# A seven-product feed-forward for the second batch, with GpSimd adding the W quarters

## The chip, the cores and the metric

The kernel runs on one NeuronCore of a Trainium2 chip. The metric is the device time of one execution in microseconds (us); lower is better. PE is TensorE, DVE is VectorE, ACT is ScalarE, POOL is GpSimd and SP is the engine whose queue issues most of the DMAs. L12 is line 12 of the kernel file; a number above 1875 is always a line of the changed file.

## The reference, cut to what matters

Two batches of 1024 tokens with 2048 features go through a quantised cross-attention product and then a feed-forward product with LoRA terms. Both have the same residual form.

```python
x = x + fake_quant(layernorm(x)) @ fake_quant(ctx)             # per batch: (1024 x 2048) @ (2048 x 2048)
y = layernorm(x)
x = x + y @ W + bias + (y @ A_eff[b].T) @ B_eff[b].T + (y @ A_shared.T) @ B_shared.T
# W: 2048 x 2048 f32; eight gate groups, four for each batch; rank 32
```

The feed-forward product must be more exact than one f16 product. Both y and W are split into a high and a low f16 part, and three products are summed: high*high, high*low and low*high.

## The kernel before

A batch is 8 token tiles of 128 rows. All work is written out by hand for each engine, with semaphores between them; each engine runs its list in order. One batch has two phases of 4 column blocks (512 columns, `NBLK`). Phase one is the attention product, one bf16 matmul for each of 16 k steps (L1006). Phase two is the feed-forward: for each column block and each token tile `base_group` issues 16 k steps of three f16 matmuls (L1191, L1192, L1193), and `delta` adds two matmuls for the LoRA term (L1202, L1203). That makes 4 x 8 x 16 x 3 = 1536 main matmuls in a batch, all 128x128 by 128x512. `lora_in` (L1214) makes the rank-64 product of y four times in a batch, with 32 matmuls of 256 columns each.

Each token tile has its own of the 8 PSUM banks. `evict1` (L1464) and `evict2` (L1503) on DVE add a finished bank, scaled, to the residual `x2` in SBUF.

y is made tile by tile. DVE takes statistics (L1471, L1476), an inverse root (L1344 to L1347) and the scaled rows into `xn` (L1486); ACT copies the high part (`split_hi`, L750); DVE subtracts to get the low part (`low2`, L1496); SP issues a transposing DMA of each into `lhs` (L357, L365).

W comes in pieces of 128 x 2048 f32 (1 MB) through `stage`, which holds two pieces. The load of a piece waits until the piece two places earlier has been converted (`load_w`, L458). ACT writes the high part into `ring` (L774) and DVE the low part (L1450). One column block is 4 pieces, and each of the 16 pieces is loaded once in a batch. The LoRA rows `b_st` take the same way through `stage` (L482, L484, L781, L1456).

POOL adds the attention's column term to the residual (L613), loads a row of bias into `bias_sb` for each column block (L631), adds it to the 8 tiles (L638), and issues the stores of the output (L644, L699). Its list for a block is: bias row, eight additions, eight stores.

Of the kernel before, what the change touches and what calls it, by code (L numbers as in the profile page):

```python
# [15 lines left out]
P = 128  # L16
# [13 lines left out]
def build(nc, x, ctx_in, par, w, bias, lora_a, lora_b, lora_as, lora_bs, out):  # L30
# [20 lines left out]
    bg_scratch = nc.dram_tensor("bg_scratch", (RANK, NGATE, D), F32, kind="Internal").ap()  # L51
    bg_rows = bg_scratch.rearrange("(q h r) g o -> (h r g) q o", h=2, q=NQ // 2)
# [7 lines left out]
    with ExitStack() as es:  # L60
# [18 lines left out]
        sc = sb("sc", [P, 116], F32)  # L79
# [53 lines left out]

        def w_first(g):
            return slot(g % 2)
# [29 lines left out]
        NEG_HALF = sc[:, 104:106]  # L165

# [89 lines left out]
        stored = sem("stored")  # L256

# [83 lines left out]

        block = es.enter_context(nc.Block())

        @block.sync
        def _(sp):
# [41 lines left out]
            def load_gates(b):  # L387

                if b == 0:
                    for n in range(NBLK):  # L390
                        sp.wait_ge(ag_dram[n], 16)
                    sp.wait_ge(be_full, 6)
                else:
                    sp.wait_ge(base_done, NBLK * TILES)
                    sp.dma_start(ash(b), lora_as).then_inc(sh_again, 16)
                sp.dma_start(a_gates, ag_scratch[:, b * GPB:(b + 1) * GPB, :, :]).then_inc(ag_in, 16)
# [96 lines left out]

            for b in range(NBATCH):
                if b:
                    load_ctx(b, 0, [0, 1])
                    for t in range(5):
                        turn_next(b, t)
                    load_ctx(b, 0, [2])
                    turn_next(b, 5)  # L500
                    load_ctx(b, 0, [3])
                    turn_next(b, 6)
                    turn_next(b, 7)
                    load_ctx(b, 1, [0, 1])
                    load_gates(b)
                    load_ctx(b, 1, [2, 3])
                    with sp.Fori(2, NBLK) as j:
                        ctx_block(b, j)
                w_block(b, 0)
# [31 lines left out]
        def _(pool):  # L541
# [73 lines left out]
            def store_a(b, gs):  # L615

                for g in gs:
                    pool.wait_ge(a_lo, b * (GPB + 1) + g + 2)
# [28 lines left out]
            bias_row = bias.rearrange("(a n) -> a n", a=1)  # L647
            for b in range(NBATCH):
# [12 lines left out]
                else:  # L661
# [6 lines left out]
                    add_column(b, 3)  # L668
                add_bias(b, 0, blk2(b, 0), False)
# [33 lines left out]
        def _(act):  # L703
# [154 lines left out]
            def shared_hi(b):  # L858
                if b:
                    act.wait_ge(sh_again, 16)  # L860
# [5 lines left out]
                for n in range(2):  # L866
                    last = act.activation(a_f16[:, n, :, RANK:R2], ash(b), ACT.Copy, scale=SA)
# [13 lines left out]


# [16 lines left out]
            for b in range(NBATCH):  # L899
# [37 lines left out]
                for j in range(1, NBLK):  # L937
# [12 lines left out]
                    if j == 2:  # L950
                        gate_hi(b, 2)
                        gate_hi(b, 3)

# [42 lines left out]
        def _(pe):  # L996
# [220 lines left out]

            for b in range(NBATCH):
                if b == 0:
                    first_block()  # L1220
                for j in range(0 if b else 1, NBLK):
                    first_by_tile(b, j)
                k = blk(b, 1, 0)
# [75 lines left out]
        def _(dve):  # L1299
# [159 lines left out]
            def evict1(b, j, t):  # L1459
                dve.wait_ge(psum_full, blk(b, 0, j) * TILES + t + 1)  # L1460
                if b:
# [3 lines left out]
                                         op0=ALU.mult, op1=ALU.add).then_inc(evicted, 1)  # L1465

# [60 lines left out]
            def evict_and_convert(b, j):  # L1527
# [23 lines left out]
                if b == 0 and j == 1:  # L1551
                    power_a()
                if b == 0 and j == 2:
# [11 lines left out]
                if j == 2:  # L1565
                    gate_low(b, 2)
# [47 lines left out]
            def shared_low(b):  # L1614

                dve.wait_ge(a_hi, b * (GPB + 1) + 1)
                for n in range(2):
                    last = dve.scalar_tensor_tensor(out=a_f16[:, n, :, R2 + RANK:2 * R2], in0=ash(b), scalar=SA,
# [3 lines left out]
            def gate_low(b, g):  # L1622

                dve.wait_ge(a_hi, b * (GPB + 1) + g + 2)
# [104 lines left out]

            for b in range(NBATCH):  # L1730
                for j in range(NBLK - 1):
# [6 lines left out]
                    if b == 0 and j == 2:  # L1738
                        max_of_first_w(2)

# [86 lines left out]
                if b + 1 < NBATCH:  # L1827
                    steps[0] += LAP * (NBLK - 3)
                    for t in range(LNL, TILES):
# [46 lines left out]
```

## Time and profile before

| what | before |
|---|---|
| median of 3 runs | 1051.88 us (1051.62 to 1055.79) |
| profiled execution | 1053.82 us, span 1052.3 us |
| PE busy | 996.7 us, 95% of the span |
| DVE / ACT / POOL busy | 537.4 / 305.5 / 209.8 us |
| DMA moved | 181.70 MB |
| first feed-forward matmul of the second batch | 676.73 us |

The span is the time from the first to the last instruction in the profile. A matmul's entry overlaps the next one's, so the distance between starts tells the pace, not the duration shown.

### The profile page before, as it was taken

The numbers are of one execution on the slowest core, as the hardware profiler recorded it, in microseconds if no ns is written. First come the engines' busy times: TensorE is split into PE (matmuls) and PEld (weight loads), VectorE is DVE, ScalarE is ACT, GpSimd is POOL, SyncE is SP. The second block draws the span as 40 slices with busy tenths as digits, with TensorE's granted clock in tenths as the row PEclk, the third lists the DMA queues.
The fourth block names the chain that finished last, engine by engine and source line by source line (L and its number), as shares of the span: only waits on it lengthen the run. The fifth ranks groups of instructions, "written<-read, shape, count | busy, mean of one in ns | idle before, by whom it ended". The sixth has DMA issues, their size and how long they took to land.

```text
span 1052.3 us, 12182 instructions
## 1 busy us (share of the span) xinstructions
PE 996.7 (95%) x4736; PEld 470.0 (45%) x4759; DVE 537.4 (51%) x761; ACT 305.5 (29%) x234; POOL 209.8 (20%) x231
## 2 busy tenths in 40 slices
PE   2899999999999999999999999989999999999996
PEld 1364444444544444444444344445544444444442
DVE  7766869878364565454414756787442023014010
ACT  4684423444031142132213521353330021012000
POOL 3011000111014013113311634320204004003110
PEclk9999999999999999999999999999999999999998
DMA  9699862679465245447699743665824025014010
GB/s 364 235 312 390 319 271 46 170 143 214 153 221 201 79 160 189 164 156 199 253 293 292 290 181 129 145 143 125 229 101 160 31 98 162 20 33 156 10 46 24
DMA packets 124392, 181.70 MB, mean 173 GB/s; under 512 B 96064, under 2 KB 96064, under 8 KB 111808
## 3 DMA queue, kind: packets, MB, share of 16 engines
q1 hardware_dynamic: 109600, 118.25, 37.9%
q0 software_dynamic: 13600, 58.73, 15.2%
q10 hardware_dynamic: 1152, 4.19, 1.0%
q8 instruction: 25, 0.41, 0.2%
q14 instruction: 15, 0.12, 0.0%
HBM read 128.72 MB, written 29.36 MB: 150 GB/s over the span
## 4 chain that ended last, share of the span: by engine, by line
PE 67%; DVE 11%; DMA 8%; issue 5%; ACT 5%; SPq 2%; POOL 2%; DVEq 0%; POOLq 0%; ACTq 0%
PE psum L1191 16%; PE psum L1193 16%; PE psum L1192 16%; PE psum L1006 14%; DMA stage<-in_w 2%; PE psum L1214 2%; PE psum L1071 1%; DVE hl L1496 1%; DMA stage<-in_ctx_in 1%; DMA xn<-in_x 1%; SPq L365 1%; DMA lhs<-hl 1%; DMA bias_sb<-in_bias 1%; DVE ring L1450 1%; PE psum L1202 1%
## 5 line engine op out<-in xcount | busy, mean ns | idle before, releaser
L1191 PE MATMUL psum<-ring,lhs 128*128 128x512 f16 x1016 | 386.4, 380 | 9.1 <-issue 6.0
L1192 PE MATMUL psum<-ring,lhs 128*128 128x512 f16 x1016 | 386.3, 380 | 0.0
L1193 PE MATMUL psum<-ring,lhs 128*128 128x512 f16 x1016 | 386.3, 380 | 0.0
L1006 PE MATMUL psum<-ring,lhs 128*128 128x512 bf16 x1002 | 228.7, 384 | 4.5 <-DVE ring L1416 2.0
L1191 PEld LDWEIGHTS psum<-ring,lhs 128*128 128x128 f16 x1016 | 99.6, 98 | 131.0 <-issue 8.4
L1006 PEld LDWEIGHTS psum<-ring,lhs 128*128 128x128 bf16 x1024 | 100.9, 99 | 127.8 <-issue 7.4
L1193 PEld LDWEIGHTS psum<-ring,lhs 128*128 128x128 f16 x1016 | 99.6, 98 | 120.7 <-issue 1.4
L1192 PEld LDWEIGHTS psum<-ring,lhs 128*128 128x128 f16 x1016 | 99.7, 98 | 119.6 <-issue 1.4
L1503 DVE SCALAR_TENSOR_TENSOR x<-psum,sc,x 128x512 f32<-128x512 f32 (+1 forms) x64 | 45.3, 745 | 180.4 <-PE psum L1203 179.5
L638 POOL TENSOR_TENSOR x<-x,bias_sb 128x512 f32<-128x512 f32 (+1 forms) x64 | 89.0, 1416 | 185.7 <-ACT x L915 123.6
L774 ACT ACTIVATE ring<-stage,sc 128x2048 f16<-128x2048 f32 x32 | 63.6, 1999 | 207.7 <-PE psum L1193 159.9
L1450 DVE SCALAR_TENSOR_TENSOR ring<-stage,sc,ring 128x2048 f16<-128x2048 f32 x32 | 75.0, 2349 | 78.1 <-ACT ring L774 74.8
L762 ACT ACTIVATE ring<-stage,pats_sb,sc 128x2048 int16<-128x2048 f32 x30 | 62.5, 2089 | 88.1 <-DMA stage<-in_ctx_in 47.2
L644 POOL DMA_DIRECT2D out<-x x48 | 26.7, 556 | 237.2 <-DVE x L1503 213.6
L1464 DVE SCALAR_TENSOR_TENSOR x<-psum,sc,x 128x512 f32<-128x512 f32 x64 | 45.7, 745 | 31.7 <-PE psum L1006 13.6
L1416 DVE TENSOR_SCALAR ring<-ring 128x2048 bf16<-128x2048 int16 x30 | 26.4, 881 | 51.2 <-ACT ring L762 51.2
L613 POOL TENSOR_TENSOR x<-x,bias_sb 128x512 f32<-128x512 f32 x32 | 45.4, 1454 | 27.8 <-ACT bias_sb L911 27.8
L1456 DVE SCALAR_TENSOR_TENSOR b_st<-stage,sc,b_st 64x1024 f16<-64x1024 f32 x16 | 21.7, 1356 | 53.6 <-ACT b_st L781 53.5
L750 ACT ACTIVATE hl<-xn 128x2048 f16<-128x2048 f32 x16 | 30.6, 1910 | 48.8 <-DVE xn L1486 44.0
L1334 DVE BATCH_NORM_STATS2 stats<-xn 128x6 f32<-128x512 f32 x32 | 19.8, 681 | 44.6 <-DMA xn<-in_x 44.5
L1496 DVE TENSOR_TENSOR hl<-xn,hl 128x2048 f16<-128x2048 f32 x16 | 36.9, 2307 | 7.7 <-DMA lhs<-hl 7.5
L781 ACT ACTIVATE b_st<-stage,sc 128x1024 f16<-128x1024 f32 x16 | 18.4, 1147 | 69.2 <-DMA stage<-in_lora_bs 69.2
(167 smaller groups left out, 675.1 us busy)
## 6 DMA issues: line engine op xcount, KB each, us to landing
stage<-in_w SPq DMA_DIRECT2D x38, 1024.0 KB, 6.3
stage<-in_ctx_in SPq DMA_DIRECT2D x30, 1024.0 KB, 7.4
out<-x POOLq DMA_DIRECT2D x64, 256.0 KB, 3.5
x<-in_x POOLq DMA_DIRECT2D x8, 1024.0 KB, 11.9
xn<-in_x POOLq DMA_DIRECT2D x8, 1024.0 KB, 7.0
x<-in_x POOLq DMA_DIRECT2D x4, 2048.0 KB, 15.0
lhs<-in_lora_a POOLq DMA_DIRECT2D x4, 1024.0 KB, 12.7
lhs<-in_lora_b SPq DMA_DIRECT2D x4, 1024.0 KB, 8.9
```

The costliest lines, as they stand in the source:

```text
L613: pool.tensor_tensor(v, v, bias_sb[:, :], ALU.add).then_inc(with_col, 1)
L638: pool.tensor_tensor(v, v, bias_sb[:, :], ALU.add).then_inc(biased, 1)
L762: act.activation(ring_i[:, g, j % 2, :, :], stage[:, i % 2, :, :], ACT.Relu, bias=Z2, scale=IS2).then_inc(act_conv, 1)
L774: act.activation(ring[:, g, 0, :, :], stage[:, i % 2, :, :], ACT.Copy, scale=of_block(CW0, j)).then_inc(act_conv, 1)
L1006: last = pe.matmul(psum[:, t, :], lhs_q[:, k, t * P:(t + 1) * P], ring_q[:, g, j % 2, u, :], start=(k == 0), stop=(k == KT - 1 and not by_pe))
L1191: pe.matmul(psum[:, t, :], hi, ring[:, g, 0, u, :], start=(kk == 0), stop=False)
L1192: pe.matmul(psum[:, t, :], hi, ring[:, g, 1, u, :], start=False, stop=False)
L1193: last = pe.matmul(psum[:, t, :], lo, ring[:, g, 0, u, :], start=False, stop=False)
L1450: dve.scalar_tensor_tensor(out=ring[:, g, 1, :, :], in0=stage[:, half_w(b, g), :, :], scalar=of_block(CW0, j), in1=ring[:, g, 0, :, :], op ...
L1464: dve.scalar_tensor_tensor(out=v, in0=psum[:, t, :], scalar=S12, in1=v, op0=ALU.mult, op1=ALU.add).then_inc(evicted, 1)
L1496: dve.tensor_tensor(hl[:, 1, :], xn[:, :], hl[:, 0, :], ALU.subtract).then_inc(y_lo, 1)
L1503: dve.scalar_tensor_tensor(out=v, in0=psum[:, t, :], scalar=of_block(INVS0, j), in1=v, op0=ALU.mult, op1=ALU.add).then_inc(evicted, 1)
```

## The change

The first batch and both attention phases stay as they are, but for a few small additions in the second batch: bn_stats right behind each eviction, differences of the A matrices (`split_gates`), and one common scale of W. The second batch's feed-forward is replaced. y and W are cut into quarters (512 tokens x 1024 features, 1024 x 1024) and the 2x2 block product is made with seven quarter products in place of eight. A product m is 8 PSUM banks (4 token tiles x 2 column blocks), each with 8 k steps of three matmuls.

- The y operands are sums and differences of quarters, 28 "units" (f16, high and low side by side), made by ACT, DVE and POOL. 12 of them are transposed straight into `lhs`; 16 are saved in DRAM (`y_scratch`) and transposed from there later, four at a time, in `turn_saved`.
- The W operand is a quarter for products 0 and 1 (two 1 MB pieces for each column half n). For products 2 to 6 it is the sum or difference of two quarters, made in `stage` by POOL (`w_sums`): four pieces for each n, each of them two loads of 512 KB, a POOL addition, an ACT conversion and a DVE conversion. LoRA rows take two more places in `stage` for products 2, 3, 5 and 6.
- Most products are added to two output quarters, so a bank is read twice by DVE (`out_first`, `out_second`); LoRA deltas are added by products 2 and 3 in banks of their own time (`out_delta`), and by 5 and 6 inside their bank.
- Bias and stores go by output quarter (`bias_quad`), on POOL, between the W sums.

In the diff's core, `load_use` is SP's, `w_sums`, `bias_quad` and the first `products` are POOL's, `product_bank` is PE's and `late_product` is DVE's.

```diff
+        W_OF = [((1, 1),), ((0, 0),), ((1, 0), (0, 0)), ((0, 1), (1, 1)), ((0, 0), (1, 1)), ((0, 0), (0, 1)), ((1, 0), (1, 1))]
+        W_USE = [(0, 2), (4, 6), (8, 14), (18, 24), (28, 32), (36, 42), (46, 52)]
+        B_USE = {2: 12, 3: 22, 5: 40, 6: 50}
...
+            def load_use(f):
+                if f < 2:
+                    sp.wait_ge(act_conv, act1(1, NBLK - 1, f + 2) + 1)
+                else:
+                    sp.wait_ge(converted, CONV0 + f - 1)
...
+            def w_sums(m, n):
+                for i in range(4):
+                    f = W_USE[m][n] + i
+                    pool.wait_ge(stage_in[f % 2], in_stage(f))
+                    v = stage[:, f % 2, 0:2, :]
+                    pool.tensor_tensor(v, v, stage[:, f % 2, 2:4, :], W_OP[m]).then_inc(w_sum_pool, 1)
+
+            def bias_quad(place, half, c, done, first, store_too):
+                for n in range(2):
...
+                    pool.wait_ge(biased_quad, nth * PT)
+                    pool.dma_start(bias_sb[:, :], bias_row[:, j * NW:(j + 1) * NW].to_broadcast([P, NW])).then_inc(bias_row_in, 16)
+                    pool.wait_ge(bias_row_in, 16 * (nth + 1))
+                    for t in range(PT):
+                        pool.wait_ge(done, first + n * PT + t + 1)
+                        v = x2[:, half * PT + t, j * NW:(j + 1) * NW]
+                        pool.tensor_tensor(v, v, bias_sb[:, :], ALU.add).then_inc(biased_quad, 1)
+                        if store_too:
+                            pool.wait_ge(biased_quad, nth * PT + t + 1)
+                            pool.dma_start(out_v[1][:, half * PT + t, j, :], v).then_inc(stored, 16)
+
+            def products():
+                for p in range(PT):
+                    pair_sums(p)
+                w_sums(2, 0)
+                w_sums(2, 1)
+                pool.wait_ge(with_col, NBLK * TILES)
+                w_sums(3, 0)
+                w_sums(3, 1)
+                bias_quad(0, 1, 0, out_d, 0, True)
+                w_sums(4, 0)
+                w_sums(4, 1)
+                bias_quad(1, 0, 1, out_d, 8, True)
+                w_sums(5, 0)
+                w_sums(5, 1)
+                bias_quad(2, 0, 0, out_a, 8 * 4, False)
+                w_sums(6, 0)
+                w_sums(6, 1)
+                bias_quad(3, 1, 1, out_a, 8 * 5, True)
+                for n in range(2):
+                    for t in range(PT):
+                        pool.wait_ge(out_a, 8 * 6 + n * PT + t + 1)
+                        pool.dma_start(out_v[1][:, t, n, :], x2[:, t, n * NW:(n + 1) * NW]).then_inc(stored, 16)
...
+            def product_bank(m, t, n):
+                bank = 2 * t + n
+                q = quad(QUAD_OF[m])
+                for h in range(2):
+                    if t == 0:
+                        w_in_ring(m, n, h)
...
+            def late_product(m):
...
+                half_parts(m, 1, 0)
+                out(0)
+                out(1)
+                half_parts(m, 1, 2)
+                out(2)
+                out(3)
+                if m + 1 < PRODUCTS:
+                    half_parts(m + 1, 0, 0)
+                out(4)
+                if m + 1 < PRODUCTS:
+                    half_parts(m + 1, 0, 2)
+                    if m + 1 in (5, 6):
+                        low_delta(m + 1)
+                out(5)
+                out(6)
+                out(7)
```

The POOL list of the second batch's feed-forward, last column block of before (L631 loads the bias row, L638 adds it, L699 stores):

```order
L631 DMA bias_sb<-in_bias 128x512
L638 TENSOR_TENSOR x<-x,bias_sb 128x512 x8
L699 DMA out<-x 128x512 x8
```

The POOL list of the change from product 5's W sums (L874) on; L882 loads the bias row, L887 adds it, L890 stores:

```order
L874 TENSOR_TENSOR stage<-stage 128x1024 x8
L882 DMA bias_sb<-in_bias 128x512
L887 TENSOR_TENSOR x<-x,bias_sb 128x512 x4
L882 DMA bias_sb<-in_bias 128x512
L887 TENSOR_TENSOR x<-x,bias_sb 128x512 x4
L874 TENSOR_TENSOR stage<-stage 128x1024 x8
L882 DMA bias_sb<-in_bias 128x512
L887 TENSOR_TENSOR x<-x,bias_sb 128x512
L890 DMA out<-x 128x512
```

The sums of the next product's W now stand behind a whole output quarter's bias rows, additions and (except in this one quarter) stores.

The SP list of the second batch before, from the last tile's transposes on (L357, L365), with W pieces (L458) and the A matrices of a gate group (L492):

```order
L357 DMA_TRANSPOSE lhs<-hl 128x16x128
L365 DMA_TRANSPOSE lhs<-hl 128x16x128
L458 DMA stage<-in_w 128x2048 x2
L492 DMA ap_st<-a_scratch 128x2048
L458 DMA stage<-in_w 128x2048 x2
L482 DMA stage<-bg_scratch 32x2x512
```

The SP list of the change from the LoRA rows of product 3 (L613) to those of product 5 (L611); L595 is half a W piece, L644 a transpose from DRAM:

```order
L613 DMA stage<-in_lora_bs 32x2x512
L595 DMA stage<-in_w 128x1024 x4
L644 DMA_TRANSPOSE lhs<-y_scratch 128x16x128 x4
L595 DMA stage<-in_w 128x1024 x4
L644 DMA_TRANSPOSE lhs<-y_scratch 128x16x128 x4
L595 DMA stage<-in_w 128x1024 x8
L644 DMA_TRANSPOSE lhs<-y_scratch 128x16x128 x4
L595 DMA stage<-in_w 128x1024 x16
L611 DMA stage<-bg_scratch 32x2x512
```

Groups of four transposes now stand between loads of one product's W pieces.

## Rows read from the trace of the kernel before

**Rows 1.** The page: busy time of each engine, TensorE's clock in 40 slices
```profile
PE 996.7 (95%) x4736; PEld 470.0 (45%) x4759; DVE 537.4 (51%) x761; ACT 305.5 (29%) x234; POOL 209.8 (20%) x231
PEclk9999999999999999999999999999999999999998
```

**Rows 2.** Waits of PE from 640 us to the end
```profile
PE psum L1191 <- issue: 3.2, 1, 3.2
PE psum L1202 <- DVE ap_st L1518: 1.5, 1, 1.5
```

**Rows 3.** Timeline of PE: start, us, engine, line, operation, tiles, count, idle before
```profile
24.03 3.60 PE L1006 MATMUL psum<-ring,lhs 128*128 128x512 bf16 x8 [1.71 <-DVE ring L1416]
...
676.73 0.38 PE L1191 MATMUL psum<-ring,lhs 128*128 128x512 f16 x1
...
678.03 0.38 PE L1191 MATMUL psum<-ring,lhs 128*128 128x512 f16 x1
...
697.78 3.66 PE L1214 MATMUL psum<-lhs,ap_st 128*128 128x256 f16 x32
704.62 0.38 PE L1191 MATMUL psum<-ring,lhs 128*128 128x512 f16 x1 [3.19 <-issue]
...
707.13 0.63 PE L1193 MATMUL psum<-ring,lhs 128*128 128x512 f16 x1
707.56 0.63 PE L1191 MATMUL psum<-ring,lhs 128*128 128x512 f16 x1
```

**Rows 4.** Stretches: us, busy of PE, PEld, DVE, ACT, POOL, clock, DMA
```profile
707.00:710.00 3.00, 3.00 (x11) 1.17 (x10) 1.89 (x5) 1.42 (x2) 1.04 (x1) 0.68 0.99 198
860.00:950.00 90.00, 90.00 (x418) 40.83 (x417) 20.37 (x15) 11.76 (x7) 15.72 (x17) 1.00 0.29 96
```

**Rows 5.** Timeline of DVE around the end of the second batch's attention
```profile
654.90 0.75 DVE L1464 SCALAR_TENSOR_TENSOR x<-psum,sc,x 128x512 f32<-128x512 f32 x1 [3.27 <-POOL x L613]
...
656.78 1.87 DVE L1471 BATCH_NORM_STATS2 stats<-x 128x6 f32<-128x512 f32 x3
658.57 0.15 DVE L1344 RECIPROCAL sc<-sc 128x1 f32<-128x1 f32 x1
...
659.50 1.35 DVE L1486 TENSOR_SCALAR xn<-x,sc 128x2048 f32<-128x2048 f32 x1
...
704.62 2.29 DVE L1496 TENSOR_TENSOR hl<-xn,hl 128x2048 f16<-128x2048 f32 x1 [1.04 <-DMA lhs<-hl]
```

**Rows 6.** Groups by line and shape, 760 us to the end: busy us, mean ns
```profile
L1450 DVE SCALAR_TENSOR_TENSOR ring<-stage,sc,ring 128x2048 f16<-128x2048 f32 x12 | 28.2, 2351 | 43.7 <-ACT ring L774 43.5
L1503 DVE SCALAR_TENSOR_TENSOR x<-psum,sc,x 128x512 f32 x16 | 11.6, 748 | 97.7 <-PE psum L1203 97.7
L1456 DVE SCALAR_TENSOR_TENSOR b_st<-stage,sc,b_st 64x1024 f16<-64x1024 f32 x6 | 8.2, 1374 | 15.7 <-ACT b_st L781 15.7
L781 ACT ACTIVATE b_st<-stage,sc 128x1024 f16<-128x1024 f32 x6 | 6.9, 1148 | 22.4 <-DMA stage<-in_lora_bs 22.4
```

**Rows 7.** Timeline of POOL: an addition beside DVE's L1496, and one alone
```profile
705.79 2.25 POOL L638 TENSOR_TENSOR x<-x,bias_sb 128x512 f32<-128x512 f32 x1 [6.16 <-ACT x L915]
724.78 1.27 POOL L638 TENSOR_TENSOR x<-x,bias_sb 128x512 f32<-128x512 f32 x1 [16.74 <-ACT x L915]
```

**Rows 8.** Timeline of POOL: bias row, additions, stores
```profile
871.86 0.54 POOL L644 DMA_DIRECT2D out<-x  x1 [0.57 <-DVE x L1503]
872.64 0.54 POOL L644 DMA_DIRECT2D out<-x  x1 [0.24 <-issue]
873.97 0.54 POOL L631 DMA_DIRECT2D bias_sb<-in_bias  x1 [0.78 <-issue]
879.70 10.82 POOL L638 TENSOR_TENSOR x<-x,bias_sb 128x512 f32 x8 [5.19 <-DMA bias_sb<-in_bias]
...
1043.86 1.20 POOL L699 DMA_DIRECT2D out<-x  x2 [19.23 <-DVE x L1503]
```

**Rows 9.** DMA issues from 860 us on: count, KB, median us to landing
```profile
stage<-in_w SPq DMA_DIRECT2D x5, 1024.0 KB, 4.9
stage<-bg_scratch SPq DMA_DIRECT2D x8, 128.0 KB, 3.5
```

**Rows 10.** SP's queue: transposes from DRAM, LoRA rows; last, landing of transposes, 640 us on
```profile
558.10 5.58 SPq L439 DMA_TRANSPOSE lhs<-q_scratch  x2
...
786.88 0.33 SPq L482 DMA_DIRECT2D stage<-bg_scratch  x1
...
lhs<-hl SPq DMA_TRANSPOSE x16, 4.4
```

**Rows 11.** Timeline of ACT: the first LoRA rows of a block are read
```profile
791.10 1.15 ACT L781 ACTIVATE b_st<-stage,sc 128x1024 f16<-128x1024 f32 x1 [3.51 <-DMA stage<-in_lora_bs]
```

More of the change, by code:

```diff
@@ L508, in _ @@
                         ctx_block(b, j)
+                    products()
+                    continue
                 w_block(b, 0)
@@ new lines, in conv_parts, with conv_delta @@
+            def conv_parts(m, n, uses):
+                for i in uses:
+                    conv_part(m, n, i)
+            def conv_delta(m):
+                for n in range(2):
+                    f = B_USE[m] + n
+                    act.wait_ge(stage_in[f % 2], in_stage(f))
+                    if n == 0 and DELTA_NO[m] < 2:
+                        v = TILES + 5 * PT - (1 if m == 2 else 4)
+                        act.wait_ge(unit_out[v % 4], unit_done(v))
+                    elif n == 0:
+                        act.wait_ge(delta_done, 8 * (DELTA_NO[m] - 1))
+                    act.activation(b_bufs[DELTA_NO[m] % 2][:, 2 * n:2 * n + 2, :], stage[:, f % 2, 0:2, :], ACT.Copy,
+                                   scale=CB_ALL).then_inc(act_conv, 1)
@@ new lines, in lora_sum @@
+            def lora_sum(i):
+                g = GATE_ORDER[i]
+                bank = SUM_BANK[i]
+                t0 = g % 2 * TPG
+                pe.wait_ge(a_in, 16 * (GPB + i + 1))
+                if i == 3:
+                    pe.wait_ge(p_ready, GPB + 1)
+                else:
+                    pe.wait_ge(out_b, at(1, bank // 2, bank % 2) + 1)
+                for t in range(t0, t0 + TPG):
+                    if g >= 2:
+                        unit_ready(TILES + 5 * t)
+                    else:
+                        pe.wait_ge(late_in[t], 16)
+                first, second = (quad(0), quad(1)) if g >= 2 else (quad(3), quad(2))
+                for kk in range(KT):
+                    for h in range(2):
+                        src = (first if kk < HK else second)[:, h * HK + kk % HK, t0 * P:t0 * P + GT]
+                        last = pe.matmul(psum[:, bank, 0:GT], a_st[:, kk, :], src, start=(kk == 0 and h == 0),
+                                         stop=(kk == KT - 1 and h == 1))
+                last.then_inc(ax_done, 1)
@@ L1730, in _, with products @@
+            def products():
+                units_and_two_products()
+                third_product()
+                for m in range(3, PRODUCTS):
+                    late_product(m)
             for b in range(NBATCH):
```

643 lines of the change are left out of this document (634 added, 9 removed).

## The prediction, made before the changed kernel was run

> **What bounds the kernel now.** The page comes first: PE is busy 95% of the span, and its clock is full in 39 of 40 slices [rows 1]. Then the waits of PE: from 640 us to the end they come to 4.7 us [rows 2], and a 90 us stretch is all PE at full clock, with DVE, ACT and POOL each busy less than a quarter of it [rows 4]. So the second batch's feed-forward is PE's own pace. That pace is read from starts: two L1191 six matmuls apart start 1.30 us apart [rows 3], 0.216 us each. A removed matmul is worth 0.216 us as long as everything else still arrives in time, and that has to be shown for each thing that feeds PE.
>
> **What is removed.** 7 products x 8 banks x 24 matmuls = 1344 in place of 1536: 192 x 0.216 = 41.5 us less. The 64 LoRA matmuls (13.8 us) and the four rank products (3.66 us each, 14.6 us) [rows 3] stay. A bank takes 5.18 us, a product 41.5, with its 16 deltas 44.9.
>
> **Added: the y units, first two products.** DVE's list from its first eviction of the last attention block (654.90 [rows 5]) to its last eviction of product 0 is: 8 evictions with statistics, 1.88 each (654.90 to 656.78); 8 inverse roots, 1.3 each (four steps take 0.93, 658.57 to 659.50; two steps more); 36 subtractions or sums of 128x1024, half of L1496's 2.29, 1.15 each; 4 scaled tiles of 1.35 [rows 5]; 8 low parts of W, 2.35 each, and 16 output additions, 0.75 each [rows 6]. Sum: 15.0 + 10.4 + 41.4 + 5.4 + 18.8 + 12.0 = 103 us, so 758 without a wait. Every unit goes from ACT to DVE and three in seven from POOL to ACT to DVE; walking the list I count some 12 us of such waits, hence 770. PE starts product 0 at 676.9 (676.73 before) and needs unit 24 and a bank freed late in that list for the sixth bank of product 1. Following both lists, PE waits 6.4 us for W's second half in product 0 (eviction and units stand ahead of its low part on DVE), 2.8 + 1.7 in product 1, and 12 at that sixth bank: 23 us. If DVE never waited this would be 11.
>
> **Added: products 2 and 3.** Four transposes from DRAM stand ahead of W pieces on SP. Two such took SP 5.58 us [rows 10]; four take 11, and their landings (4.4 us each [rows 10]) fill the engines. (a) Product 2's second half of k waits for them: 8 us. (b) The first rank product needs product 1's last bank read, which stands on DVE behind the LoRA rows of product 2: 8 us. (c) The second and third rank products need A loads that stand on SP behind W loads which wait for conversions: 7 us. (d) In product 3 the same four transposes again: 7 us, less what (a) has moved, so 0 to 7; I take half. Sum 26, bounds 10 and 35. PE's own work up to the W pieces of product 3's second half is 676.9 + 3 x 41.5 + 14.6 + 3.5 (8 deltas) + 20.7 (4 banks) + 2.6 = 842.8. POOL's last W sum for product 3 ends at about 842.8 + 23 + 26 = **892**, less about 2 as the sum precedes the matmul: 890.
>
> **Added: the W pieces.** In products 2 to 6 a piece goes: load, POOL sum, ACT, DVE, and the next load into that half of `stage` waits for DVE. Prices: load 4.9 us [rows 9] and 0.3 for SP's issue, 5.2; POOL sum of 128x1024, not in the trace, twice the 1.27 of a 128x512 addition alone [rows 7], 2.5 (bounds 2.4 and 3.5, the latter with DVE beside it); ACT 1.15 [rows 6]; DVE 1.28, taken between half of L1450 (1.18) and the 1.37 of L1456 [rows 6].
>
> Does POOL's sum run beside DVE's low part? POOL's addition at 705.79 took 2.25 us and not 1.27; DVE's L1496, with both inputs in SBUF, held on until 706.91, 1.12 us into it [rows 5, 7]. So the one waits for the other, wholly. The low part of a W piece has two inputs in SBUF as well: the first piece's low part waits for the second piece's sum to end. A pair of pieces then takes sum 2.5 + ACT 1.15 + wait 1.3 + DVE 1.28 + load 5.2 = 11.5 us with handoffs. Without that wait it would be 10.2 and the whole forecast 12 us lower (nine pairs).
>
> The Trainium skill says it as a rule (SBUF — State Buffer, Who interferes with whom): the port pair that VectorE and GpSimd share is an exclusive lock, and whichever comes first keeps it for its whole instruction. By that rule the sum is the 11.5 us of a pair, and the trace's 2.25 us agrees; a shared bandwidth would give a value between the two.
>
> POOL's W sums of a product, from its first: four pairs are 3 x 11.5 + 5.0 = 39.5. In product 4 four transposes stand between (SP): 3 more, 42.5. In 5 and 6 the LoRA rows use `stage` between: load 4.2 (issue 786.88 [rows 10], ACT reads at 791.10 [rows 11]) and ACT, DVE: 7.3, together 46.8.
>
> **Moved: bias and stores.** `bias_quad` stands in POOL's list ahead of the next product's sums. Bias row: issue 873.97 to addition 879.70, 5.8 us; an addition 1.35 (eight in 10.82); a store 0.54 and 0.25 of gap [rows 8]. Two rows and 8 of each: 11.6 + 8 x 2.15 = 28.8; without stores (third quarter) 22.4. Before, this was hidden: nothing on POOL fed PE. Now W of the next product waits for it. Behind POOL stands ACT's conversion, behind that DVE's low part, and behind DVE the next load.
>
> A product's cycle on POOL is thus 71.3 (product 4: 42.5 + 28.8) and 69.2 (5: 46.8 + 22.4), against 44.9 of PE. PE follows: from the first sum of product 5 its first half of k is ready at 7.7, its second at 19.2, the last piece at 49, and the product ends at 69: just inside the cycle. So POOL's serial list is the bound from product 3 on.
>
> **The sum.** 890 + 28.8 (first quarter's bias) = 919; + 71.3 = 990; + 69.2 = 1059, first sum of product 6; + 46.8 + 28.8 (last bias) = 1135; + 6.1 (eight last stores, 0.76 each) = 1141; + 7.2 from the last issue to the span's end (1045.1 to 1052.3 [rows 8]) = **1148 us**. The profiled time is 1.5 above its span, the median 1.9 below the profiled time, so the span stands for the median. That is 96 us or 9% slower.
>
> Bounds: sums at 2.4, no lock, bias rows at 5, no waits of (d): 1105. Sums at 3.5 and 12 us more of stalls: 1190.
>
> **The rivals.**
> A. The forecast, POOL's list is the bound: 1105 to 1190.
> B. POOL gets through its bias faster than rows say (its stores and additions fall in the waits for W loads after all): a cycle is then 45 to 47, as the W pipeline alone sets. 890 + 42.5 + 2 x 46.8 + 28.8 + 13.3 = 1068; 1055 to 1100. Against it: POOL's list is in order, and the bias stands between sums of two products, not between pieces.
> C. Faster. POOL keeps up and PE's pace bounds: 676.9 + 290.3 + 13.8 + 14.6 + 9.5 of tail = 1005, and 1050 with the early stalls. It decides where a cycle on POOL, sums and bias, is under 44.9; at the rows' prices the sums alone are 39.5 to 46.8. It also needs most of the 49 us of early stalls to be gone, or it only equals before.
> D. The clock. After 3.19 us of idling PE ran eight matmuls at 0.43 us, and in that stretch the granted clock was 0.68; early in the kernel, after longer gaps, eight took 3.60 [rows 3, 4]: the 1.2 GHz level against 2.4. In A, PE idles some 8 us at each product and shorter at each half. If it came back only late, a product would take 208 x 0.427 = 89 us and not 69: 20 more, three times, some 1200. For one dip of 4 us it costs 2 us, and A has room for it.
>
> The Trainium skill (TensorE: Matmul & The Clock Gate, The HAM clock gate) holds that the slow level is the default and activity earns the fast one. By that rule every long wait of A is followed by a slow stretch, as after 701.43 in this trace; it is D only if the clock stays down.
>
> **How the numbers follow.** A 0.79, B 0.08, C 0.06 (0.04 faster, 0.02 within 0.5%), D 0.05, and 0.02 for a still slower mishap. The time is A's, 1148. The range 1090 to 1192 holds nearly all of A and a little of B and D. A difference under 0.5% is about what a measurement of this kernel can't tell from none: faster 0.04, same 0.02, slower 0.94.
>
> **What would show it.** In the profile after: POOL's L874 2.4 to 2.8 us each (3.5 or more where DVE's low part is beside it); four blocks of 22 to 29 us of bias between them; the first L874 of products 4, 5 and 6 near 919, 990 and 1059; PE waiting on DVE's `ring` at the start of each of the last three products, 10 to 25 us each; `stage` loads 5 us. The prediction is wrong if L874 comes at or under 1.5 us, if POOL idles for W loads more than it works, if product 0 to 3 take over 230 us or under 180, or if PE has no gap over 5 us after 890.

## The result, and the profile after

The changed kernel takes 1180.43 us in the median of 4 runs (1177.46 to 1182.75), the kernel before on the same chip 1053.26 (4 runs, 1051.62 to 1055.79). The ratio is 1.120, with a 95% interval of 1.117 to 1.124: 12% or 127 us slower. The forecast was 1148, 96 slower. The profiled span is 1181.2 us, and forecasts below are held against that execution.

First the page, the lines that answer to [rows 1]: busy time, POOL in tenths of 40 slices (29.5 us each), TensorE's clock.

```profile
PE 992.9 (84%) x4544; PEld 458.9 (39%) x4567; DVE 705.8 (60%) x928; ACT 365.8 (31%) x296; POOL 343.1 (29%) x287
...
POOL 3011001110131131320333403471313453626354
PEclk9999999999999999999889998878799878869797
```

PE is busy about as long as before with 192 matmuls fewer, as part of them ran at a lower clock; what the span has more is idle time. Both begin at slice 20 (560 us), ahead of the feed-forward. Where before PE waited 4.7 us from 640 us on [rows 2], the waits of PE from 690 us to the end are (us in total, times, longest):

```profile
PE psum L1656 <- DVE ring L2389: 61.5, 11, 9.7
PE psum L1656 <- DVE x L2409: 23.5, 3, 13.6
PE psum L1695 <- DVE x L2409: 13.1, 1, 13.1
PE psum L1718 <- DMA ap_st<-a_scratch: 7.5, 2, 6.4
PE psum L1718 <- issue: 5.5, 1, 5.5
PE psum L1695 <- DVE hl L2403: 4.1, 1, 4.1
PE psum L1695 <- DVE b_st L2403: 2.2, 1, 2.2
```

117 us of waits. L2389 is DVE's low part of a W piece, L2409 its read of a finished bank. The waits name DVE, but DVE is only the last link. By stage (columns as in [rows 4]: us, busy of PE, PEld, DVE, ACT, POOL, clock, DMA):

```profile
694.00:800.00 106.00, 75.60 (x315) 32.27 (x316) 104.02 (x102) 62.28 (x47) 46.21 (x14) 0.86 0.69 201
800.00:930.00 130.00, 106.45 (x516) 52.94 (x514) 68.69 (x81) 23.84 (x24) 34.12 (x15) 0.91 0.65 184
930.00:1181.00 251.00, 171.95 (x706) 72.38 (x706) 82.33 (x83) 32.45 (x29) 120.48 (x95) 0.83 0.52 164
```

In products 0 and 1 DVE has no pause (104 of 106 us), though some 27 us of that it stands behind POOL's additions (the last section has the rows). From 930 us on no engine is busy all the time, which is what a serial chain looks like on a page. The chain is seen on POOL's timeline between product 3 and product 4 (start, us, ..., idle before, releaser):

```profile
923.21 2.34 POOL L874 TENSOR_TENSOR stage<-stage 128x1024 f32<-128x1024 f32 x1 [10.81 <-DMA stage<-in_w]
926.80 2.34 POOL L874 TENSOR_TENSOR stage<-stage 128x1024 f32<-128x1024 f32 x1 [1.25 <-DMA stage<-in_w]
929.08 0.58 POOL L882 DMA_DIRECT2D bias_sb<-in_bias  x1
933.65 1.26 POOL L887 TENSOR_TENSOR x<-x,bias_sb 128x512 f32<-128x512 f32 x1 [3.99 <-DMA bias_sb<-in_bias]
935.20 0.56 POOL L890 DMA_DIRECT2D out<-x  x1 [0.30 <-POOL x L887]
...
948.81 1.26 POOL L887 TENSOR_TENSOR x<-x,bias_sb 128x512 f32<-128x512 f32 x1 [5.92 <-DMA bias_sb<-in_bias]
...
957.39 4.64 POOL L874 TENSOR_TENSOR stage<-stage 128x1024 f32<-128x1024 f32 x2
```

No piece of W is summed from 929.1 to 957.4. Behind it, in order, wait ACT, DVE and PE:

```profile
959.78 1.15 ACT L1178 ACTIVATE ring<-stage,sc 128x1024 f16<-128x1024 f32 x1 [29.46 <-POOL stage L874]
```
```profile
960.96 3.58 DVE L2389 SCALAR_TENSOR_TENSOR ring<-stage,sc,ring 128x1024 f16<-128x1024 f32 x2 [25.37 <-ACT ring L1178]
964.45 2.06 DVE L2409 SCALAR_TENSOR_TENSOR x<-psum,sc,x 128x512 f32<-128x512 f32 x3
```
```profile
966.00 0.59 PE L1695 MATMUL psum<-hl,ap_st 128*128 128x512 f16 x1 [13.08 <-DVE x L2409]
```

The last row is one that I had not foreseen: in `late_product` the first low parts of product 4 stand ahead of the last bank reads of product 3, so POOL's bias holds up the end of product 3 as well. It costs nothing of its own, as POOL's list is what bounds here.

Each milestone of the forecast's sum, beside what the trace has:

| place | forecast | measured | off so far |
|---|---|---|---|
| first feed-forward matmul | 676.9 | 694.26 | +17.4 |
| sixth bank of product 1 starts (67.3 of matmuls, 23 of waits) | 767.2 | 798.92 | +31.7 |
| last W sum of product 3 ends | 890 | 929.1 | +39.1 |
| first sum of product 4 | 919 | 957.4 | +38.4 |
| first sum of product 5 | 990 | 1028.5 | +38.5 |
| first sum of product 6 | 1059 | 1093.4 | +34.4 |
| end | 1148 | 1181.2 | +33.2 |

The whole error lies before product 4. POOL's cycles, the reason for the forecast, came near: 71.2 us against 71.3, then 64.8 against 69.2, then 87.8 against 88.9.

### The profile page after: what moved, and what is told of

It is laid out like the page before. It is cut to its first block, busy times and chain, and to the rows that moved or that the text cites. A ratio compares the mean times of both kernels' runs of the same rounds, so it can differ in the third digit from the quotient of the medians.

```text
span 1181.2 us, 12067 instructions
## 1 busy us (share of the span) xinstructions
PE 992.9 (84%) x4544; PEld 458.9 (39%) x4567; DVE 705.8 (60%) x928; ACT 365.8 (31%) x296; POOL 343.1 (29%) x287
## 4 chain that ended last, share of the span: by engine, by line
DVE 25%; DMA 24%; PE 16%; POOL 10%; issue 9%; ACT 8%; SPq 7%; DVEq 0%; POOLq 0%; ACTq 0%
DMA stage<-in_w 10%; PE psum L1430 9%; DMA bias_sb<-in_bias 5%; POOL x L887 3%; POOL stage L874 3%; SPq L644 3%; DMA xn<-in_x 3%; DVE ring L2389 3%; DMA stage<-in_lora_bs 2%; DMA stage<-in_ctx_in 2%; POOL x L846 2%; DVE hl L2343 2%; DVE x L2024 2%; ACT ring L1178 1%; DVE ring L1976 1%
## 5 line engine op out<-in xcount | busy, mean ns | idle before, releaser
L1656 PE MATMUL psum<-ring,lhs 128*128 128x512 f16 x448 | 181.1, 404 | 85.0 <-DVE ring L2389 61.5
L1430 PE MATMUL psum<-ring,lhs 128*128 128x512 bf16 x1002 | 231.9, 387 | 15.4 <-DVE ring L1976 12.7
L1615 PE MATMUL psum<-ring,lhs 128*128 128x512 f16 x508 | 193.3, 381 | 5.0 <-DVE ring L2010 2.8
L1617 PE MATMUL psum<-ring,lhs 128*128 128x512 f16 x508 | 193.3, 380 | 0.0
L1616 PE MATMUL psum<-ring,lhs 128*128 128x512 f16 x508 | 193.1, 380 | 0.0
L2389 DVE SCALAR_TENSOR_TENSOR ring<-stage,sc,ring 128x1024 f16<-128x1024 f32 (+1 forms) x48 | 86.9, 1819 | 171.7 <-ACT ring L1178 170.0
L1657 PE MATMUL psum<-ring,lhs 128*128 128x512 f16 x448 | 180.5, 403 | 0.0
L1658 PE MATMUL psum<-ring,lhs 128*128 128x512 f16 x448 | 180.2, 402 | 0.0
L874 POOL TENSOR_TENSOR stage<-stage 128x1024 f32<-128x1024 f32 x40 | 99.0, 2480 | 183.5 <-DMA stage<-in_w 183.3
L1178 ACT ACTIVATE ring<-stage,sc 128x1024 f16<-128x1024 f32 (+1 forms) x48 | 61.4, 1288 | 254.4 <-POOL stage L874 240.3
L1656 PEld LDWEIGHTS psum<-ring,lhs 128*128 128x128 f16 x448 | 46.1, 103 | 149.8 <-issue 56.9
L2409 DVE SCALAR_TENSOR_TENSOR x<-psum,sc,x 128x512 f32<-128x512 f32 x112 | 76.6, 743 | 19.9 <-PE psum L1696 11.7
L1615 PEld LDWEIGHTS psum<-ring,lhs 128*128 128x128 f16 x508 | 49.8, 98 | 66.3 <-DVE ring L2010 4.3
L846 POOL TENSOR_TENSOR x<-x,bias_sb 128x512 f32<-128x512 f32 (+1 forms) x32 | 43.6, 1386 | 109.3 <-ACT x L1333 64.1
L1617 PEld LDWEIGHTS psum<-ring,lhs 128*128 128x128 f16 x508 | 49.9, 98 | 60.4 <-issue 0.8
L1616 PEld LDWEIGHTS psum<-ring,lhs 128*128 128x128 f16 x508 | 49.9, 98 | 59.7 <-issue 0.8
L1658 PEld LDWEIGHTS psum<-ring,lhs 128*128 128x128 f16 x448 | 46.1, 103 | 60.1 <-issue 12.8
L1657 PEld LDWEIGHTS psum<-ring,lhs 128*128 128x128 f16 x448 | 46.0, 103 | 57.3 <-issue 11.4
L1976 DVE TENSOR_SCALAR ring<-ring 128x2048 bf16<-128x2048 int16 x30 | 31.7, 1057 | 54.9 <-ACT ring L1032 54.8
L2024 DVE SCALAR_TENSOR_TENSOR x<-psum,sc,x 128x512 f32<-128x512 f32 x64 | 46.3, 744 | 16.8 <-PE psum L1465 11.8
```

The costliest lines, as they stand in the source:

```text
L874: pool.tensor_tensor(v, v, stage[:, f % 2, 2:4, :], W_OP[m]).then_inc(w_sum_pool, 1)
L1178: act.activation(dst, src, ACT.Copy, scale=CW_ALL).then_inc(act_conv, 1)
L1430: last = pe.matmul(psum[:, t, :], lhs_q[:, k, t * P:(t + 1) * P], ring_q[:, g, j % 2, u, :], start=(k == 0), stop=(k == KT - 1 and not by_pe))
L1615: pe.matmul(psum[:, t, :], hi, ring[:, g, 0, u, :], start=(kk == 0), stop=False)
L1616: pe.matmul(psum[:, t, :], hi, ring[:, g, 1, u, :], start=False, stop=False)
L1617: last = pe.matmul(psum[:, t, :], lo, ring[:, g, 0, u, :], start=False, stop=False)
```

## The experiments

The first eight were run once each, beside one run of the kernel before (1055.4 for e1 to e4, 1057.3 for e5 to e8); the last four are medians of four, beside 1054.55. A single run tells no less than some 3 us (the changed kernel's four lie within 5.3). The span is 1.5 us under each profiled time.

**e1. No bias on POOL.** Is the bias block between the W sums what bounds?

```diff
-                    pool.dma_start(bias_sb[:, :], bias_row[:, j * NW:(j + 1) * NW].to_broadcast([P, NW])).then_inc(bias_row_in, 16)
-                    pool.wait_ge(bias_row_in, 16 * (nth + 1))
...
-                        pool.tensor_tensor(v, v, bias_sb[:, :], ALU.add).then_inc(biased_quad, 1)
+                        k = nth * PT + t
+                        pool.memset(xn[:, k:k + 1], 0.0).then_inc(biased_quad, 1)
```

> This kernel leaves out the second batch's bias rows and bias additions (a one-column memset keeps the order), stores stay. Theory A, POOL's serial list of W sums and bias bounds products 3 to 6: a bias block falls from 28.3 us to about 7.5 (stores alone), the third from 17 to 1, so the time falls by about 79 us, to about 1101. Theory B, the loads through the two halves of stage bound the pieces by themselves and the bias mostly fills waits: the cycles stay at 60 us or more and the time at 1150 or more.

Measured: 1142.7, 38 less, half of what theory A said. POOL shows why: what was left of the block ended at 937, and then

```profile
949.18 4.82 POOL L874 TENSOR_TENSOR stage<-stage 128x1024 f32<-128x1024 f32 x2 [12.08 <-DMA stage<-in_w]
```

The sums now wait for W loads, which stand on SP behind four transposes (919.93 to 938.19). Product 4's first sum comes at 949.18, 8 us before the changed kernel's 957.39, where the shorter block alone would have given 20. Product 5's comes 54.7 us later in place of 71.2, which is the whole of its shorter block; product 6's 53.9 in place of 64.8, with 7 us of waiting for a W load where the block was. From product 6's first sum to the end only 4 us are won, and there the last stores wait for PE's last banks. So the bias block was the bound, and the supply of W pieces is a second one, 8 us behind it at product 4.

**e2. The sums of products 3 to 6 on VectorE.** This takes POOL out of the W chain altogether.

```diff
             def half_parts(m, n, i0):
+                for i in (i0, i0 + 1) if m >= 3 else ():
+                    f = W_USE[m][n] + i
+                    dve.wait_ge(stage_in[f % 2], in_stage(f))
+                    v = stage[:, f % 2, 0:2, :]
+                    dve.tensor_tensor(v, v, stage[:, f % 2, 2:4, :], W_OP[m]).then_inc(w_sum_pool, 1)
```
(and the calls of `w_sums` for these products are left out of POOL's list)

> The W sums of products 3 to 6 go to VectorE, everything else stays. Theory A: the bias blocks no longer stand ahead of W pieces; a pair of pieces takes about 9 us, a product 45 to 50, and the time is 1100 to 1125. Theory B (the loads bound by themselves): a product stays over 60, the time over 1150. Theory C, VectorE becomes the bound with its added 9.6 us a product: a product 55 or more and PE waiting for output additions.

Measured: 1137.7, 43 less, 13 short of the hoped for. For the last half of product 3's W PE waits 16.37 us, at 937.26, where the changed kernel waits 7.22 at 931.70. The group of DVE's sums, 860 us to the end:

```profile
L2390 DVE TENSOR_TENSOR stage<-stage 128x1024 f32<-128x1024 f32 x32 | 43.3, 1358 | 82.1 <-DMA stage<-in_w 82.1
```

1.36 us a sum against POOL's 2.4, and 82 us of waits for loads. e1 and e2 end within 5 us of each other, from opposite edits, which is what a common second bound would give; e9 tests it.

**e3. Eight additions more in the second bias block.** The opposite of e1: if POOL's list is the bound, what is added has to appear in the time.

```diff
+                        if place == 1:
+                            w = xn[:, t * NW:(t + 1) * NW]
+                            pool.tensor_tensor(w, w, w, ALU.add)
```

> Eight extra 128x512 additions on GpSimd, into a buffer that nobody reads, in the second bias block (between the W sums of products 4 and 5). Theory A: all of it is on the path, 8 x 1.3 = 10 to 11 us more, about 1191. Theory B: 0 to 3 us more, as the next W pieces are late anyway.

Measured: 1183.05, only 2.6 above the changed kernel's median and within what one run can't tell. But this run began its feed-forward at 687.6, not 694.3, and its first sum of product 4 came at 951.1, 6.3 us earlier. From there to the first sum of product 5 it took 78.2 us against 71.2, 7 more (the eight additions took 1.03 to 1.05 us each, 8 in all and not the 10 to 11 that I had said), and PE's wait for product 5's W was 16.4 us at 1036.53 against 9.55 at 1035.84. The added time is on the path, nearly whole; the total alone would have told nothing. Why this one started earlier than its likes was not settled: it is 6 us ahead already at 576.14, where a row of POOL's additions begins (582.09 in the changed kernel). e10 has what moves the start in the main.

**e4. One load less ahead of the second batch's feed-forward.** The feed-forward began 17.4 us late. One suspect was the added second load of the shared A.

```diff
-                    sp.dma_start(ash_upper, lora_as).then_inc(sh_again, 16)
```

> The second load of the shared A matrix, issued while the second batch's first attention block waits for its loads, is left out (the LoRA term is then wrong). Theory D: that load and what it pushes back made the second batch's feed-forward start at 694.3 us and not at 676.7; the start goes back by 10 us or more and the time to 1165 to 1170. Theory E: it starts late for another reason (the port pair, or transposes that happened to be slower); the start moves by under 3 us.

Measured: start at 693.49 against 694.26, total 1176.9, little more than one run's 3 us away. That theory falls. (The kernel leaves out a load that the LoRA term needs.)

**e5 and e6. Transposes dealt out one by one between the W loads**, with the sums on POOL (e5) and on VectorE (e6).

```diff
-                load_parts(3, 1, range(2))
-                turn_saved(3, 4, 1)
-                load_parts(3, 1, range(2, 4))
-                turn_saved(2, 5, 2)
-                load_parts(4, 0, range(4))
+                for i in range(4):
+                    load_part(3, 1, i)
+                    turn_saved(3, 4, 1, [i])
+                for i in range(4):
+                    load_part(4, 0, i)
+                    turn_saved(2, 5, 2, [i])
```

> The groups of four transposes from DRAM are dealt out one by one between W pieces. Theory A2: a group of four holds the next W piece up on SP and in the DMA engines (gaps before a W sum of 19.3, 13.3 and 11.8 us where others are 6 to 7), so the time falls by 15 to 20 us, to 1161 to 1166, and these gaps come down to 8 or less. Theory F: the transposes' DMA time is what costs and it is only shared out: less than 5 us.

> The same, with the W sums of products 3 to 6 on VectorE. If the transposes are what held the kernel with VectorE sums at 1138 (PE waited 16.4 us at once for the second half of product 3), 1115 to 1122. If VectorE itself bounds it there, 1132 or more.

Measured: 1175.7 and 1132.6, 5 less than each one's partner (the changed kernel and e2), not much over what one run can tell. A group of four had held SP's queue (start, us), and a load behind it waited:

```profile
903.18 14.30 SPq L644 DMA_TRANSPOSE lhs<-y_scratch  x4
917.54 2.00 SPq L595 DMA_DIRECT2D stage<-in_w  x4
919.64 16.37 SPq L644 DMA_TRANSPOSE lhs<-y_scratch  x4
936.06 2.10 SPq L595 DMA_DIRECT2D stage<-in_w  x4
```

Dealt out, the same transposes still pass through the same queue, and most of the gain that was hoped for did not come.

**e7. All of the bias in one load.** The eight bias rows become one early load of 1 MB into `xn`, which is idle by then; additions and stores stay. That takes the two row waits, but nothing else, out of each bias block.

```diff
+                pool.wait_ge(unit_lo, TILES + 5 * PT)
+                pool.dma_start(xn[:, :], bias_row.to_broadcast([P, D])).then_inc(bias_row_in, 16)
                 w_sums(2, 1)
...
-                        pool.tensor_tensor(v, v, bias_sb[:, :], ALU.add).then_inc(biased_quad, 1)
+                        pool.tensor_tensor(v, v, xn[:, j * NW:(j + 1) * NW], ALU.add).then_inc(biased_quad, 1)
```

> All four bias rows come in one load into a buffer that is free by then; the additions and stores stay on GpSimd. Theory A: eight waits from issue to first addition, 3.3 to 6.5 us each and 32.6 in all, leave the list; the first quarter's part is taken over by the late W load, so 18 to 25 us less, 1156 to 1163. Theory B (W loads bound anyway): under 8 us less.

Measured: 1155.8, 25 less, as theory A said, though 3.4 us of it are an earlier start (690.89 against 694.26). The bias blocks are 18.4, 18.4, 11.8 and 18.4 us, and first sums of products come 63.0 and 60.8 apart, in place of 71.2 and 64.8.

**e8. e6 and e7 together.**

> Spread transposes, W sums of products 3 to 6 on VectorE, one bias load. If GpSimd's list is off the path once the sums have left it, this equals the kernel without the bias change within 5 us.

Measured: 1146.6, not equal to e6 but 14 slower. Half is there by 936.66, where PE gets the last half of product 3's W (929.65 in e6): the rank products of product 2, beside which the 1 MB load runs, waited 8.35, 7.03 and 1.99 us against 5.68 and 6.92 in e6. (1.4 us of it are a later start.) In e7, which has the same load, the three waited 7.25, 7.68 and 0.68 against the changed kernel's 5.50, 6.41 and 1.12. The other half comes later, while DVE's sums take 1511 ns against 1320. What makes them longer was not isolated. Taking a wait off POOL has no worth once POOL is off the path, and its load then seems to have a price, which no run here isolates.

**e9. A third place for W pieces**, on e6. `xn` (as large as half of `stage`) takes every third piece from product 3 on, so a load waits for the conversion three places back.

```diff
+        def at_place(f):
+            return f % 2 if f < THIRD else f % 3
+        def place(f):
+            return xn[:, :].rearrange("p (a n) -> p a n", n=NW) if at_place(f) == 2 else stage[:, at_place(f), :, :]
...
-                    sp.wait_ge(converted, CONV0 + f - 1)
+                    sp.wait_ge(converted, CONV0 + f - (1 if f < THIRD + 2 else 2))
```

> Turns spread and the sums on VectorE as in the sixth run (1132.6 us), and from product 3 on a third place for W pieces (the memory of xn, which is idle by then), so that a piece's load waits for the conversion of the piece three places back, not two. The sixth run's VectorE waited 62.5 us for W loads from 940 us on, in 44 loads of 5.6 us each. If it is the turn of a place (load, sum, two conversions, next load) that bounds the W pieces, this run is 10 to 25 us faster: 1108 to 1122 us. If it is what the DMA engines deliver (about 194 GB/s in that stretch) or the engines' own work, the two stay alike: 1128 or more.

Measured: 1110.2, 22 less than e6. PE's waits for DVE's ring from 690 us on fall from 41.2 to 29.9 us, those at the LoRA rows from 7.2 to 0.2, and the DMA engines move 219 GB/s in the last 190 us where e6 moved 194. So the second bound was the turn of a place: load, sum, two conversions and only then the next load.

**e10. The common scale of W worked out later.** The one thing that the change adds to DVE ahead of the second batch is `scale_of_all`, seven operations on one column in front of the last tiles' statistics (497.11 to 502.27 in the changed kernel's trace).

```diff
-                    scale_of_all()
                     for t in range(LNL, TILES):
                         norm_next(b + 1, t)
...
                     for t in range(6, TILES):
                         evict2(b, NBLK - 1, t)
+                    scale_of_all()
```

> The changed kernel with one thing moved: the common scale of W (seven small VectorE instructions) is worked out behind the last evictions of the first batch, not ahead of the last tiles' statistics. If it is what starts the second batch's attention late, the first feed-forward matmul comes 4 to 8 us earlier (686 to 690 in place of 694.3) and the whole is 1172 to 1176 us. If the late start has another cause, nothing moves by over 2 us.

Measured: first feed-forward matmul at 681.01 (13.3 earlier, more than I had said) and 1168.3 in all, 12 less. Five microseconds of tiny operations cost thirteen. They are not even five by themselves: in e10, at 567.62 to 568.92, the seven take 0.15 or 0.16 us each, 1.3 in all. In the old place a row of eight POOL additions runs beside them (493.50 to 504.32), and each of the four with two inputs takes nearly an addition's time:

```profile
497.11 1.11 DVE L2319 TENSOR_TENSOR sc<-sc 128x1 f32<-128x1 f32 x1
498.26 1.19 DVE L2320 TENSOR_TENSOR sc<-sc 128x1 f32<-128x1 f32 x1
499.48 1.19 DVE L2321 TENSOR_TENSOR sc<-sc 128x1 f32<-128x1 f32 x1
500.70 0.15 DVE L2322 TENSOR_SCALAR sc<-sc 128x1 f32<-128x1 f32 x1
500.89 1.00 DVE L2323 TENSOR_TENSOR sc<-sc 128x1 f32<-128x1 f32 x1
```

DVE and POOL of the changed kernel at 577 us, then of e10:

```profile
577.03 0.69 DVE L1976 TENSOR_SCALAR ring<-ring 128x2048 bf16<-128x2048 int16 x1 [4.55 <-ACT ring L1032]
...
581.75 10.72 DVE L1976 TENSOR_SCALAR ring<-ring 128x2048 bf16<-128x2048 int16 x1 [4.02 <-ACT ring L1032]
582.09 9.82 POOL L821 TENSOR_TENSOR x<-x,bias_sb 128x512 f32<-128x512 f32 x8
```
```profile
576.09 0.69 DVE L1976 TENSOR_SCALAR ring<-ring 128x2048 bf16<-128x2048 int16 x1 [3.28 <-ACT ring L1032]
...
577.64 11.56 POOL L821 TENSOR_TENSOR x<-x,bias_sb 128x512 f32<-128x512 f32 x8
579.27 0.75 DVE L2024 SCALAR_TENSOR_TENSOR x<-psum,sc,x 128x512 f32<-128x512 f32 x1 [1.23 <-POOL x L821]
```

The quantising of the last tiles came some 5 us later, their transposes on SP too (one begins at 516.38, its like at 510.79 in e10), and the context loads behind them; then the conversion L1976, which feeds PE, fell together with POOL's eight additions and sat behind all of them, 10.7 us for a 0.69 us operation. In e10 it had gone by 1.5 us before, and POOL's row itself came some 4.5 us earlier. PE's waits for L1976 from 500 us on, 10.5 us in the changed kernel, are gone in e10. e12 starts at 680.88 as well; the ten other kernels, with the scale in its old place, start between 687.6 (e3) and 695.8. In all of these and in the changed kernel a DVE operation sits through the whole row: L1976, or the one behind it (in e1, e3, e8 and e11), 10.0 to 11.5 us. In e10 and e12 none does.

**e11 and e12. The third place with POOL's sums, and everything at once.** e11 is e5 with e9's edit; e12 is e9 with e10's edit.

> The fifth run (turns spread, sums on GpSimd, 1175.7 us) with the third place. GpSimd's eight sums of a product take 46 to 49 us there and 20 us of it is work; the rest is waiting for loads. If those waits are the turn of a place, eight sums come to 30 to 40 us and the run to 1140 to 1158. If they are the rate of the DMA engines, 1168 or more.

> The ninth run and the tenth's move together. The two act in different places (before 690 us and after 860), so the gains add if both are there: the ninth run's time less 0 to 8 us. Still slower than the kernel before, which is 1055: some 50 us or more.

Measured: e11 1154.1 (1141.9 to 1159.5), 22 less than e5, inside the range given. POOL's waits for W loads from 860 us on (both of its places) come to 97.3 us against 132.7 in e5. e12 is 1099.9 (1094.6 to 1110.8), 10 less than e9, where I had allowed up to 8: the gains add. It is the best version made here and still 4.7% slower than the kernel before (interval 3.9 to 5.4%), so no version beats it. Its waits of PE, 690 us to the end:

```profile
PE psum L1665 <- DVE ring L2398: 28.2, 5, 7.4
PE psum L1665 <- DVE x L2423: 23.2, 3, 12.4
PE psum L1727 <- DMA ap_st<-a_scratch: 6.6, 1, 6.6
PE psum L1727 <- issue: 5.5, 1, 5.5
```

63.5 us of waits. From its first feed-forward matmul (680.88) to PE's last (1083.72) are 402.8 us: 318.7 of matmuls, 63.5 of waits, and 20.6 left for the half-speed stretches behind them. The kernel before has 366.1 there. The waits alone eat the 41.5 us saved.

## Why the forecast was right, and where it was off

- **The mechanism (rival A) was right and is shown.** POOL's serial list bounded products 4 to 6: less in a bias block gave less (e1, e7), more gave more (e3), by about the amounts of the list until another bound came. The list is in good part waiting, too: of the 46 to 49 us of a product's eight sums only 20 are work, the rest is waiting for W loads, and e11, which shortens that, is 22 us faster than e5 with the bias where it was. Rival C (faster) asked for a cycle under 44.9 us; none came under 64.8.
- **Terms of the list.** L874 at 2.48 us (2.5 forecast); 46.4, 47.7 and 49.0 us of sums in a product (42.5, 46.8, 46.8), as the transposes and the rank rows cost more than I gave them; bias blocks of 28.3, 24.9 and 17.1 (28.8, 28.8, 22.4), as the bias rows of the second and third block kept POOL waiting 2.8 to 3.3 us each and not 5.2. In product 4's cycle the two errors cancel, which is luck; in the later ones the shorter blocks are worth up to 4 us more.
- **Rival B fell** in its own form: no bias work slid into the load waits. But its W pipeline was nearer than I held. I had put its cycle at 45 to 47 us, far under POOL's 71; with the bias gone (e1, stores left) first sums came 54.7 and 53.9 us apart, and with the sums off POOL's list altogether (e2) 54.1 and 52.2.
- **The step that failed: "PE start of product 0 at 676.9 (676.73 before)".** I took everything ahead of the feed-forward as unchanged, though the change adds `scale_of_all` and statistics to DVE there. It was 17.4 late; 13.3 of it is the scale (e10). For the 4.1 left, PE's waits for reads of banks in the attention, 5.1 us in e10 against 2.2 before, are the only sign; the statistics behind each eviction are the likely cause, which was not tried.
- **Mis-sized: the stalls of products 0 and 1.** 6.68, 5.10, 4.78 and 13.58 us are 30.1 in place of 23. I had priced all 36 of DVE's unit operations at 1.15 us, as if alone, and counted the lock between DVE and POOL only for the W pieces. But POOL's own additions for the units run beside them: 14 of the 28 subtractions L2343 took 2.1 to 3.4 us in place of 1.2, and the 28 together 60.5 us, some 27 more than at 1.21 each. DVE's hand-over waits, which I had put at 12 us, came to 2 from 694 to 800 us and gave part of that back. I had left the clock out of it as well. After a wait matmuls start 0.43 us apart for a while, as the rows below show (the first matmul after the longest wait, and the pace after it); 104.7 us from the first matmul to the sixth bank are 67.4 of matmuls, 30.1 of waits and 7.1 of the low clock.

```profile
798.92 0.59 PE L1656 MATMUL psum<-ring,lhs 128*128 128x512 f16 x1 [13.58 <-DVE x L2409]
799.30 0.63 PE L1657 MATMUL psum<-ring,lhs 128*128 128x512 f16 x1
799.73 0.63 PE L1658 MATMUL psum<-ring,lhs 128*128 128x512 f16 x1
...
801.87 0.40 PE L1657 MATMUL psum<-ring,lhs 128*128 128x512 f16 x1
802.11 0.38 PE L1658 MATMUL psum<-ring,lhs 128*128 128x512 f16 x1
```

- **Products 2 and 3: the sum of the stalls was right, and what it lacked is the clock.** PE waited 4.99, 5.50, 6.41, 1.12 and 7.22 us up to 931.70, where it gets product 3's last W pieces: 25.2 in place of 26. In the parts it was less right: (a) was put at 8, (b) at 8, (c) at 7 and (d) at 3.5, and four transposes held SP for 14.3 to 16.4 us, not 11. But from the sixth bank (798.92) to 931.70 are 132.8 us, of which 98.6 are matmuls at full pace and 25.2 waits; 9.0 are left, the half-speed stretches behind the waits. With the 7.1 of products 0 and 1 the clock cost 16 us ahead of product 4, some 2.3 for each of its seven dips. I had priced one dip at 2 us (rival D) and put none into the sum. So PE's 39.7 us behind the forecast (931.70 against 892) are 17.4 of late start, 7.1 of stalls and 16.1 of clock, less 0.8.
- **The clock (rival D).** Full pace was back after seven matmuls at half speed behind the longest wait (798.92 to 801.87) and after 5.8 us behind that at 977.06: it did not stay down. It goes between the 2.4 GHz level and 1.2, and the mean granted clock from 930 us on is 0.83. From the first feed-forward matmul to PE's last (1164.63) are 470.4 us: 318.7 of matmuls at full pace, 117.4 of waits and 34.3 left, nearly all of it clock. That the slow level is where PE falls back to when it idles is what the Trainium skill holds (TensorE: Matmul & The Clock Gate, The HAM clock gate), and the rows agree.
- **My own list of signs.** L874 was not under 1.5 us, and PE had gaps over 5 us after 890, as said. "If POOL idles for W loads more than it works" was closer than I thought: 84.2 us of such waits against 105.7 busy from 957 us on, but 137.5 against 137.4 from 860. One sign tripped: products 0 to 3 "over 230 us or under 180". They took 234.8 us up to the last W sum and 272.6 to product 4's first matmul (966.81). The bound was set too low even for my own sum, which has 213 us up to that sum and some 23 more behind it.
- **The range.** 1180 lies in A's 1105 to 1190, but not for A's reasons: the upper end stood on sums of 3.5 us, which came at 2.48, and on 12 us more of stalls. The late start and the clock, which no bound had in it, used that room. That part is luck.

## What to carry to other kernels

Count an algorithm that saves matmuls by what it adds to the list of each engine that feeds them, in program order: here seven products for eight saved 41.5 us of PE and put a bias block in front of each product's weights. Remove one serial bound and look for the next right behind it, before believing the first one's whole price; a buffer more (e9) was worth as much as a whole bias row scheme (e7). And what a change adds ahead of its main part, however tiny, is priced by who runs beside it and who stands behind it: seven one-column operations of 1.3 us took 5 beside POOL's additions and cost 13.

## What the runs showed of the hardware

**DVE and POOL take turns, a whole instruction at a time.** The forecast's lock was taken from one addition; the y units show it cleanly:

```profile
719.78 3.40 POOL L862 TENSOR_TENSOR lhs<-lhs,xn 128x1024 f32<-128x1024 f32 x1 [39.63 <-DVE xn L2361]
720.88 3.39 DVE L2343 TENSOR_TENSOR hl<-xn,hl 128x1024 f16<-128x1024 f32 x1
...
723.13 3.34 POOL L864 TENSOR_TENSOR xn<-xn,lhs 128x1024 f32<-128x1024 f32 x1
```

POOL's operation alone takes 2.34 us and DVE's of that size about 1.2. DVE's begins at 720.88, can run only when POOL's is through at 723.2, and ends 1.1 us later; POOL's next begins at 723.13, stands for that 1.1 us and ends 2.2 after it. The Trainium skill (SBUF — State Buffer, Who interferes with whom) says that the pair of ports is a lock held for a whole instruction, and this agrees to some 0.15 us.

**Who gets the lock next is another matter.** L1976 (one input, 16-bit) sat through eight additions of POOL one after the other, 10.72 us, though its row begins 0.34 us before theirs, and POOL's took 1.23 us each as if alone. The two-input operation behind it fared the same in e3 (11.39 us). In e10 DVE's operations got their turns in the same kind of run: POOL's eight took 11.56 us, and L1976, in the midst of them, 1.06 us. Both outcomes are in the kernel before too (4.68 and 1.11 us). What decides it no run here isolates; an operation that feeds PE is best kept away from a row of POOL's additions.

**A DMA transpose holds the queue that issues it.** Four took 14.30 and 16.37 us of SP's queue, where four W loads took 2.00.
